# New order of calls on all five engines' instruction lists in a macaron block (feed-forward, state space, feed-forward) on one Trainium2 core

## The reference

```python
x = x + 0.5 * ffn(layernorm(x))        # part A
x = x + mamba(layernorm(x))            # part B
x = x + 0.5 * ffn(layernorm(x))        # part C

ffn(x):   down( silu(x @ wg.T) * (x @ wu.T) )      # 256 -> 768 -> 256, int weights / 127
mamba(x): x_in, z = split(x @ in_proj.T)           # 256 -> 2 x 512
          xc = causal depthwise conv, 4 taps, + bias
          dt_r, Bm = parts of xc @ x_proj.T        # 16 and 128 columns
          delta = clip(softplus(dt_r @ dt_w.T + b), 0.001, 0.1)
          h_t = exp(delta A) h_(t-1) + (exp(delta A) - 1) / A * Bm
          y = h @ C.T + xc * D ;  out = (y * silu(z)) @ out_proj.T
```

## Time and profile before

| | us |
|---|---|
| median of 3 runs | 528.62 (527.6 to 529.53) |
| profiled execution | 528.05 |
| its span, first to last instruction | 526.3 |
| busy: TensorE / VectorE / ScalarE / GpSimd | 484.6 / 386.3 / 309.2 / 240.5 |
| mean granted TensorE clock | 0.981 |

### The profile page before, as it was taken

One profiled execution on the slowest core, in us unless ns is written; L12 is line 12 of the kernel. 1 busy time (PEld: TensorE's weight loads), 2 busy tenths in 40 slices (PEclk: granted clock), 3 DMA queues, 4 the chain that ended last, 5 costly groups with the idle time before them and its releaser, 6 DMA issues.

```text
span 526.3 us, 7715 instructions
## 1 busy us (share of the span) xinstructions
PE 484.6 (92%) x2591; PEld 281.9 (54%) x2591; DVE 386.3 (73%) x799; ACT 309.2 (59%) x540; POOL 240.5 (46%) x220
## 2 busy tenths in 40 slices
PE   2879976998999999999999999999999999977976
PEld 2446423733666464745484466646574648422855
DVE  4798938688887868686877787777878585927552
ACT  5374935097655877387646764686639761746042
POOL 1232144427282547436462829172835555144233
PEclk9999987999999999999999999999999999988989
DMA  8600000032015200630033201520142004000101
GB/s 295 190 2 2 2 0 0 2 80 42 2 22 141 41 2 1 116 87 2 2 81 81 41 3 21 140 42 2 20 104 41 1 1 82 1 2 0 41 2 41
DMA packets 53817, 23.43 MB, mean 45 GB/s; under 512 B 41728, under 2 KB 52992, under 8 KB 53760
## 3 DMA queue, kind: packets, MB, share of 16 engines
q1 hardware_dynamic: 52944, 21.84, 17.6%
q10 hardware_dynamic: 816, 0.79, 0.5%
HBM read 8.99 MB, written 4.19 MB: 25 GB/s over the span
## 4 chain that ended last, share of the span: by engine, by line
PE 80%; DVE 7%; ACT 6%; issue 3%; POOL 2%; DMA 1%; SPq 0%; DVEq 0%; ACTq 0%
PE q L1739 54%; PE dp L1739 24%; POOL xcl L514 1%; DMA hh<-in_L_ffn_w_gate_dram 1%; DVE xc L1123 1%; PE tp L1633 1%; PE q L1794 1%; DVE x L1109 1%; DVE h L1101 1%; DVE xn L1048 1%; PE q L1633 1%; ACT xc L653 1%; ACT sg L716 0%; DVE wmx L1225 0%; DVE rmx L1266 0%
## 5 line engine op out<-in xcount | busy, mean ns | idle before, releaser
L497 POOL TENSOR_TENSOR hl<-h,hh 128x512 f16<-128x512 f32 x90 | 109.5, 1231 | 108.9 <-ACT hh L724 108.5
L1123 DVE SCALAR_TENSOR_TENSOR xc<-xi,cw,xc 128x512 f32<-128x512 f32 x96 | 80.3, 840 | 7.8 <-ACT xi L742 6.9
L1101 DVE SCALAR_TENSOR_TENSOR h<-sg,hsm,q 128x512 f32<-128x512 f32 x90 | 65.9, 740 | 23.9 <-PE q L1739 12.8
L716 ACT ACTIVATE sg<-q 128x512 f32<-128x512 f32 x90 | 53.3, 595 | 34.9 <-PE q L1739 34.1
L514 POOL TENSOR_TENSOR xcl<-xc,xch 128x512 f16<-128x512 f32 x32 | 45.5, 1428 | 59.8 <-ACT xch L749 59.8
L724 ACT ACTIVATE hh<-h 128x512 f16<-128x512 f32 x90 | 55.7, 626 | 15.8 <-DVE h L1101 15.7
L1739 PE MATMUL q<-xt_Bnext,wih 128*128 128x512 f16 x224 | 59.3, 379 | 0.8 <-ACT xt_Bnext L659 0.7
L1109 DVE SCALAR_TENSOR_TENSOR x<-dp,x 128x512 f32<-128x512 f32 x48 | 33.0, 687 | 34.6 <-PE dp L1739 34.6
L1739 PE MATMUL q<-xt_C,wg 128*128 128x512 f16 x192 | 51.3, 392 | 6.6 <-ACT sg L716 3.1
L1739 PE MATMUL dp<-wo,yu 128*128 128x256 f32 x256 | 56.7, 379 | 0.0
L1739 PE MATMUL dp<-wd,hh 128*128 128x256 bf16 x384 | 52.8, 273 | 0.8 <-ACT hh L697 0.4
(11 more groups left out here) (201 smaller groups left out, 791.4 us busy)
## 6 DMA issues: line engine op xcount, KB each, us to landing
x<-in_L_attn_x_dram SPq DMA_DIRECT2D x8, 512.0 KB, 4.0
out_dram<-x SPq DMA_DIRECT2D x16, 256.0 KB, 2.4
xc<-in_L_attn_in_proj_w_dram SPq DMA_DIRECT2D x1, 1024.0 KB, 11.2
hl<-in_L_ffn_w_up_dram ACTq DMA_DIRECT2D x3, 256.0 KB, 6.0
hh<-in_L_ffn_w_gate_dram SPq DMA_DIRECT2D x3, 256.0 KB, 6.6
hh<-in_L_ffn_w_down_dram SPq DMA_DIRECT2D x1, 768.0 KB, 8.3
yu<-n_L_attn_out_proj_w_dram SPq DMA_DIRECT2D x1, 512.0 KB, 5.2
yu<-in_L_attn_x_proj_w_dram SPq DMA_DIRECT2D x1, 256.0 KB, 11.6
```

Of the source, the lines that this page charges most:

```text
L497: pool.tensor_tensor(HL[g.hid(k)][:, c, :], H[:, j, :], HH[g.hid(k)][:, c, :], ALU.subtract)\
L716: act.activation(SG[:, (first + c) % 2, :], q[bank][:, :], ACT.Silu, scale=QUANT / XS)\
L1101: dve.scalar_tensor_tensor(out=H[:, first % 3, :], in0=SG[:, first % 2, :], scalar=HSM[:, c:c + 1], in1=q[bank][:, :], op0=ALU.mult, op1=A ...
L1123: dve.scalar_tensor_tensor(out=XC[s][:, m, :], in0=XI[s][:, m, k:k + TILE], scalar=CW[:, m, k:k + 1], in1=XC[s][:, m, :], op0=ALU.mult, op ...
```

## The change

Nothing is added and nothing taken out; every engine but SyncE has calls in a new order. The core of the diff:

```diff
 ORDER (half steps 1 to 6), TensorE
-("ix0", "B"), ("ix1", "B"), ("iz0", "B"), ("ix2", "B"), ...
+("ix0", "B"), ("iz0", "B"), ("ix1", "B"), ("ix2", "B"), ...
 FIRST, TensorE
-("more0", "", -1), ("gate0", "A", -1), ("gate1", "A", -1)
+("gate0", "A", -1), ("more0", "", -1), ("gate1", "A", -1)
-("iz0", "B", 0), ("gate3", "A", 0), ("iz1", "B", 0), ("iz2", "B", 0), ("up2", "A", 0),
-("xp0", "B", 0), ("up3", "A", 0), ("gate4", "A", 0), ("xp1", "B", 0), ("xd0", "B", 0), ("gate5", "A", 0),
+("iz0", "B", 0), ("iz1", "B", 0), ("gate3", "A", 0), ("iz2", "B", 0), ("up2", "A", 0),
+("xp0", "B", 0), ("up3", "A", 0), ("xd0", "B", 0), ("gate4", "A", 0), ("gate5", "A", 0), ("xp1", "B", 0),
-("down00", "A", 0), ("down01", "A", 0), ("cp3", "B", 0), ...
+("down00", "A", 0), ("cp3", "B", 0), ("down01", "A", 0), ...
-("out10", "B", 0), ("turn0", "Bnext", 0), ("out11", "B", 0), ("turn1", "Bnext", 0)
+("out10", "B", 0), ("turn0", "Bnext", 0), ("turn1", "Bnext", 0), ("out11", "B", 0)
 FINAL, TensorE
-ix0, iz0, ix1, ix2, iz1, turn0 C, ix3, iz2, turn1 C, iz3, ... xp0, xp1, xd0, gate2 ... cp3, down00, down01
+ix0, ix1, iz0, ix2, iz1, ix3, turn0 C, turn1 C, iz2, iz3, ... xp0, xd0, xp1, gate2 ... down00, down01, cp3
-("up03", "C", 8), ("turn1", "C", 8), ("gate04", "C", 8)
+("up03", "C", 8), ("gate04", "C", 8), ("turn1", "C", 8)
 GpSimd
-root(start, "A", 0); root(start, "A", 1); cast_down()
+cast_down(); root(start, "A", 0); root(start, "A", 1)
-conv_low(late, (0, 1, 2, 3)); hidden_low(late, "C", (0, 1, 2, 3, 4, 5))
+conv_low(late, (0, 1, 2)); hidden_low(late, "C", (0,)); conv_low(late, (3,)); hidden_low(late, "C", (1, 2, 3, 4, 5))
 ScalarE, half(g)
-                conv_in(g, (2,))
                 silu_z(g, (1,))
+                conv_in(g, (2,))
+                conv_begin(g, (3,))
                 conv_high(g, (0,))
-                conv_begin(g, (3,))
-                conv_in(g, (3,))
                 split_hi(g, "C", (0, 1))
+                conv_in(g, (3,))
...
                 gate(g, "A", (5,))
-                hidden_high(g, "A", (4,))
-                act.preload_act_table_set("natural_log_exp_and_others")
-                hidden_high(g, "A", (5,))
+                hidden_high(g, "A", (3, 4, 5))
                 rank_in(g)
+                act.preload_act_table_set("natural_log_exp_and_others")
                 softplus_exp(g)
                 softplus_log(g)
                 decay_relu(g)
+                input_in(g)
                 decay_exp(g)
-                input_in(g)
                 table(ACT.Silu, 4)
                 gate(g, "C", (0, 1))
-                hidden_high(g, "C", (0,))
+                hidden_high(g, "C", (0, 1))
                 gate(g, "C", (2,))
-                hidden_high(g, "C", (1,))
-                gate(g, "C", (3,))
                 hidden_high(g, "C", (2,))
-                gate(g, "C", (4, 5))
+                gate(g, "C", (3, 4))
                 hidden_high(g, "C", (3, 4))
+                gate(g, "C", (5,))
 ScalarE, start tile (late alike: preload ahead of conv_high(3))
+            act.preload_act_table_set("natural_log_exp_and_others")
             rank_in(start)
-            input_in(start)
-            act.preload_act_table_set("natural_log_exp_and_others")
             softplus_exp(start)
             softplus_log(start)
+            hidden_high(start, "A", (1,))
+            input_in(start)
             decay_relu(start)
...
 ScalarE, late: hidden_high(late, "C", (1,)) goes behind gate(late, "C", (2, 3)), input_in behind decay_relu
 VectorE, half(g)
-                stats(g, "Bnext", (0, 1))
                 decay_out(g)
                 hidden(g, "C", (0,))
                 input_out(g)
                 hidden(g, "C", (1,))
+                stats(g, "Bnext", (0, 1))
                 stats(g, "Bnext", (2, 3))
...
-                hidden(g, "C", (3, 4, 5))
-                skip_y(g, (0, 1, 2))
-                split_lo(g, "Bnext", (0,))
+                hidden(g, "C", (3, 4))
+                skip_y(g, (0,))
+                hidden(g, "C", (5,))
+                skip_y(g, (1,))
+                if ahead.has("A"):
+                    variance_tile(ahead, "A")
+                skip_y(g, (2,))
                 residual(g, "C", 0)
                 skip_y(g, (3,))
-                if ahead.has("A"):
-                    variance_tile(ahead, "A")
+                split_lo(g, "Bnext", (0,))
                 residual(g, "C", 1)
 VectorE, prologue
             weight_rows("u", 0)
+            stats(before, "A", (0, 1, 2, 3))
             weight_rows("g", 1)
             weight_rows("u", 1)
-            stats(before, "A", (0, 1, 2, 3))
...
+            flags[1] = flag_value(1)
+            further_parts(1)
             x_proj_scale(1)
-            flags[1] = flag_value(1)
             residual(before, "A", 0)
...
-            norm_lo(start, "Bnext", (0,))
             variance(first, "C", (0,))
-            norm_lo(start, "Bnext", (1,))
+            norm_lo(start, "Bnext", (0, 1))
 VectorE, late and last
             conv(late, 3, (1,))
-            hidden(late, "C", (0, 1))
+            hidden(late, "C", (0,))
             conv(late, 3, (0,))
+            hidden(late, "C", (1,))
...
             stats(last, "C", (2, 3))
+            normalize(last, "C", (0, 1))
             variance(last, "C", (1,))
-            normalize(last, "C", (0, 1, 2, 3))
+            normalize(last, "C", (2,))
             norm_lo_half(last, 0)
             hidden_half(last, 0, (0,))
             hidden_half(last, 0, (1,))
             hidden_half(last, 0, (2,))
+            normalize(last, "C", (3,))
             hidden_half(last, 0, (3,))
```

More of the change, by code:

```diff
@@ L61, in has @@
     return {"A": -1 <= h <= LAST - 2, "B": 0 <= h <= LAST - 1, "C": 1 <= h <= LAST}[part]
-ORDER = (("ix0", "B"), ("ix1", "B"), ("iz0", "B"), ("ix2", "B"), ("iz1", "B"), ("ix3", "B"), ("iz2", "B"),
+ORDER = (("ix0", "B"), ("iz0", "B"), ("ix1", "B"), ("ix2", "B"), ("iz1", "B"), ("ix3", "B"), ("iz2", "B"),
          ("iz3", "B"), ("gate0", "A"), ("up0", "A"), ("gate1", "A"), ("up1", "A"), ("gate2", "A"), ("up2", "A"),
@@ L866, in _ @@
             gate(before, "A", (4,))
-            norm_hi(start, "A", (1,))
             scale_row(2)
             scale_row(3)
-            hidden_high(before, "A", (2,))
             scale_row(4)
-            hidden_high(before, "A", (3,))
+            norm_hi(start, "A", (1,))
+            fill("d0")
+            hidden_high(before, "A", (2, 3))
             gate(before, "A", (5,))
-            fill("d0")
             fill("d1")
@@ L891, in _ @@
             norm_hi(before, "Bnext", (0, 1))
+            gate(start, "A", (2,))
             fill("c0")
             fill("o0")
-            gate(start, "A", (2,))
             conv_begin(start, (0,))
@@ L902, in _ @@
             conv_in(start, (2,))
-            hidden_high(start, "A", (0,))
             conv_begin(start, (3,))
@@ L921, in _ @@
             table(ACT.Silu, 4)
-            gate(start, "A", (4, 5))
-            hidden_high(start, "A", (2, 3))
+            gate(start, "A", (4,))
+            hidden_high(start, "A", (2,))
+            gate(start, "A", (5,))
+            hidden_high(start, "A", (3,))
             silu_z(start, (3,))
@@ L958, in _ @@
             decay_relu(late)
+            input_in(late)
             decay_exp(late)
@@ L1468, in half @@
                 stats(Half(g.h + 1), "C", (0, 1))
-                variance(Half(g.h + 1), "C", (0,))
+                carry(g)
                 if ahead.has("A"):
                     split_lo(ahead, "A", (0, 1))
+                variance(Half(g.h + 1), "C", (0,))
             first = Half(1)
@@ L1491, in _ @@
             norm_lo(before, "A", (0, 1))
-            variance(start, "A", (0, 1))
+            variance(start, "A", (0,))
             flags[0] = flag_value(0)
             further_parts(0)
+            variance(start, "A", (1,))
             weight_rows("d", 0)
@@ L1497, in _ @@
             hidden(before, "A", (0,))
-            normalize(start, "A", (2,))
+            normalize(start, "A", (2, 3))
             hidden(before, "A", (1,))
-            normalize(start, "A", (3,))
             row_scales()
+            over(1)
             hidden(before, "A", (2, 3))
@@ L1505, in _ @@
             hidden(before, "A", (4,))
-            over(1)
             norm_lo(start, "A", (1,))
@@ L1514, in _ @@
             in_proj_low(1)
+            flags[1] = flag_value(1)
+            further_parts(1)
             x_proj_scale(1)
-            flags[1] = flag_value(1)
             residual(before, "A", 0)
+            stats(before, "Bnext", (0, 1))
+            variance(before, "Bnext", (0,))
             in_proj_low(2)
-            stats(before, "Bnext", (0, 1))
+            residual(before, "A", 1)
             x_proj_unscale()
-            variance(before, "Bnext", (0,))
-            residual(before, "A", 1)
-            further_parts(1)
+            stats(before, "Bnext", (2, 3))
             in_proj_low(3)
```

(11 more changed lines are left out.)

69 lines of the change are left out of this document (34 added, 35 removed), and 20 rows, old and new, of tables (FINAL, FIRST).

## The result

The changed kernel takes 514.23 us (median of 4 runs, 513.5 to 516.88), the kernel before 528.42 beside it: ratio 0.9739, 95% interval 0.9699 to 0.9779. The forecast was 518.2 with a range of 515.0 to 524.5, so the direction held and the size did not: 4 us more came than forecast. The profiled execution took 513.5 us, its span 511.7.

The account below looks back on a forecast made before the run. TensorE, busy 92% of the span, was taken as the bound, with gains only in its waits and half clock. Terms -4.0, -0.9, -5.1 and -0.25 sum to -10.25 from 528.05: 517.8, set at 518.2 us; range 515 to 524.5.

Parts of the forecast that it names:

- Opening: 0 to 53 us: a 0.5 us lead from earlier statistics, half eaten by an earlier flag read of 1.3 us; -0.25 us.
- Start tile's recurrence: 69 to 97 us: early table load and xd0 ahead of xp1 bring down00 forward; -3.5 us, bounds -5.3 and -1.9.
- about 3 us of half clock: Start tile: TensorE at half clock for about 3 us, charged behind the 2.7 us still idle.
- (d): Rival, more gained: no half clock in the start tile, gap at cp0 closed, -1.5 and -0.9, 515.8 us; chance 0.06.
- Last product and turn: End of the start tile: turn1 ahead of out11, -0.8, low half waiting behind a variance, +0.25; -0.55 us.
- Entry, give-back 0.3: Into the first half step: VectorE's h0 leads by 4.0 us, TensorE by 4.3; new wait up to 2 us at up0.
- Six half steps: Middle: earlier GpSimd subtraction shortens the gap at cp0, less 0.2 us scan delay; -0.15 each, -0.9 us in all.
- Step 7: gate4 3.0 us earlier, and 2.1 us less from gate4 to up5 without half clock; -5.1 us, bounds -6.0 and -3.0.
- Last tile: turn0 earlier by normalize ahead of the second variance, low half waiting longer; -0.25 us, bounds -0.5 and +0.5.
- (b): Rival, slower: conv_in(3) behind the splits makes up0 wait in every half step, 12.3 us, 530.5 us; chance 0.07.
- (c): Rival, nothing gained: a reload undoes the early exp/ln load, -3.5 and -5.1 fall away, 526.8 to 528 us; chance 0.05.
- (a): Rival, half of it: a wait comes back elsewhere or the clock falls, +5.0, 523.2 us; chance 0.20.

Follow-up runs that it names:

- the first half as a whole: The kernel before with the new order up to the first down product alone; run once, 526.53 us beside 528.92.
- the start tile's part alone: The kernel before with the new order from the start tile's recurrence to the first half step alone; 523.59 us, ratio 0.991.
- the run with the useless matmuls elsewhere: The changed kernel with matmuls that nothing reads in four of TensorE's idle times, order unchanged; 511.98 us, ratio 0.9687.
- the fillers: Matmuls that nothing reads, in TensorE's idle times: 521.33 us added to the kernel before, 511.98 us added to the changed kernel.

## Why the prediction was wrong, point by point

The profiled execution gained 4.30 us more than the sum: 1.62 in the half steps, 1.42 in the start tile, 0.85 in the opening, 0.76 in the last tile and 0.40 at the entry, less 0.75 in step 7. The mechanism held in the start tile and in step 7. The terms that failed are the half clock charged behind the start tile's wait, the 0.15 us per half step, and the cost of the flag read with the value of the rest of the opening. Luck has a share: the median lies 0.8 us below the range, and of the four executions the two with mean clock 0.993 took 513.5 and 513.76 us, while one with 0.980 took 516.88, inside it.

- *Opening, -0.25 with bounds -0.8 and +0.8.* Failed. The 0.5 us lead was right (the down product starts 31.82 us behind the first transpose instead of 32.37). The 1.3 us for the flag read was not: the changed kernel's VectorE has no gap at it. And I called gate0 ahead of more0 worth nothing and did not count the early over(1) and the new places of the hidden copies, where the first half as a whole brings 1.1 to 1.3 us, with the down product's two waits gone. Which of its edits does that was not tried.
- *Start tile's recurrence, -3.5.* It gave 4.7. The mechanism was right to the row: the load hidden at 66.47, xd0 forecast at 70.6 on before's axis (measured 69.97 with 1.1 us of lead, so 71.1), the silu at 80.5 (80.85), iz3 in the gap, up4 at 80.95 (81.47), idle time 2.7 (2.90). The term that failed is "about 3 us of half clock" behind that wait. None came, in the changed kernel and in the start tile's part alone; in the run with the useless matmuls elsewhere it did. I had a bound for it, -5.3, of which up4's 0.5 us of lateness took most of the difference, and priced it in (d) at a chance of 0.06.
- *Last product and turn, -0.55.* It gave 0.76 at ix0, and behind that came the wait of 0.2 for the low half that was forecast.
- *Entry, give-back 0.3.* The new wait at up0 came as forecast, 1.80 us in the first half step only. But nothing was given back, since the earlier C split speeds VectorE: the run with conv_in(3) put back lost 0.9 us, and with the start tile's order alone 0.7 us were given back.
- *Six half steps, -0.9.* Failed in size, below its bound of -1.8: 0.40 per step instead of 0.15. The cause named, the earlier subtraction, was right. I set 0.2 us of delay for the scan against it, and missed that the same move takes GpSimd out from beside the scan, 1.85 to 1.28 us, so that it ends 0.34 us earlier against gate5.
- *Step 7, -5.1.* Right in its steps: xd0 forecast at 466.5 on before's axis (466.6), silu 474.5 (474.7), gate4 475.1 (475.35) without a wait. It gave 4.35: of the missing 0.75, 0.25 are in front of gate4, 0.14 between gate4 and cp0, and 0.36 are in the down products (0.20 of it one idle time at 474.24), which I had called TensorE's own. "The copy behind the early load loses 1.28 us" was too much: 0.3.
- *Last tile, -0.25.* It gave 1.01. Failed by the clock: the stretch at 0.66 behind turn0 did not come in the profiled execution. The order's own gain was the 0.5 us of turn0 (2.30 instead of 2.80 us of waiting).
- *Rivals.* (b) and (c) did not happen: TensorE waits on xi once, and xp1's place, not a reload, decides. (a) did not either. (d) is what came, and it was not alone: the opening and the scan lay outside its sum of 515.8.

In short: I charged the half clock as a fixed toll behind a wait near 3 us, where the same wait of 2.90 us brought it in one kernel of four; and I left the order's own gains in the half steps and the opening 2.5 us too small. The clock took 6.4 us of the kernel before. With the fillers in, the order is worth 9 to 10 us, near the 10.25 forecast, which had some clock in it.

## What to carry to other kernels

Price the clock first: add up what TensorE loses at 0.50 behind its waits (here 6.4 us of 528, as large as most edits), and forecast with and without it, since the same wait brings it in some kernels and executions and not in others. When an engine's operation shows two durations (1.28 and 1.85 us for the scan), look for the other engine's work beside it, because moving that work is a gain of its own. Two edits that cost or give little alone can close a gap together, so test them together before dropping one.
